# Heads of the stages of a two-layer decoder kernel: where stores are awaited, where semaphores are cleared, in which order weights are split, and two combinations reordered

## The chip, the core and the metric

One core of one Trainium2 chip runs the kernel. A core has a matmul engine (TensorE, PE in the rows), a vector engine (VectorE, DVE), a scalar engine (ScalarE, ACT), a general one (GpSimd, POOL) and one that issues DMA transfers (SyncE, SP); each has a queue of its own, and they wait for each other on semaphores. The metric is the device time of one execution in microseconds (us), lower is better.

## The reference

It computes two decoder layers over 2048 tokens of 512 numbers, here 16 batches of 128 tokens. Cut to its last lines:

```
x = _layernorm(x + _L0_attn_ref(x, ...))    # 16 heads of 128, rope, causal
x = _layernorm(x + _L0_xattn_ref(x, ctx_1024, fside, fside, ...))   # 32 heads of 16, axial rope
x = _layernorm(x + _L0_ffn_ref(x, ...))     # 32 experts, top 4, capped at 80 tokens, and a shared expert
x = _layernorm(x + _L1_attn_ref(x, ...))    # 16 heads of 32, causal
x = _layernorm(x + _L1_xattn_ref(x, ctx_1024, ...))   # 16 heads of 128, rms norm of q and k
x = _layernorm(x + _L1_ffn_ref(x, ...))     # 8 experts of 352, top 2
```

The attentions look across the tokens of groups of batches; the routed experts read packed rows of tokens and write rows, which are gathered back, weighted and summed (the combination) before the layer norm.

## The kernel before

The kernel is a row of stages, each an `nc.Block()` of its own with five instruction streams, buffers and semaphores. In the order in which they run, with the names that prefix their tiles: **a** (`wide_attention` with rope), **b** (`narrow_attention` with rope and the first router), **cd** (`late_routing`, with a part of the shared expert), **m** (`capped_experts`), **cc** (`combine_beside`: the rows of the routed experts gathered and summed, beside three quads of four batches of the shared expert on PE), **d** (`narrow_attention`, causal), **e** (`wide_attention` with rms norms and the second router), **r** (`end_of_routing`), **n** (`routed_experts`) and **fc** (`combine_last`).

Every product of fp32 matrices is made of three matmuls of halves: a number is split into a high half (a cast, `w_hi`, `x_hi`) and the rest (a subtraction, `w_lo`, `x_lo`), and `split_product` (lines 87 to 89; line 1263 in the narrow stages) multiplies high by low, low by high and high by high. So before the first product of a stage, its weights and its first row of tokens must be loaded and split. The 128x512 row x is turned by four transposes on PE (`turn_x`, lines 637 and 1253), copied and cast by ACT (lines 318, 326, 923), and its low half is made by POOL (line 392) or DVE (line 1114). Casts of weights are line 214 and 939, subtractions line 220 and, on DVE, 1123, on POOL 1043. While a head waits, PE makes `keep_busy` transposes of the identity (line 76), whose counts are the argument `busy`.

Weights of the next stages are fetched ahead by `Staged` into a shared tile `staged`; a stage with `head_ready` has its first row fetched ahead as well (`FirstTile`).

A stage ends when SP has waited for its last stores (`sp.wait_ge(out_st, ...)`); then the block's own barrier, and then `Stage.clear` at the end of the stage's context:

```
def clear(self):
    if self.used:
        self.nc.clear_and_free_semaphores(self.used)
        self.nc.all_engine_barrier()
```

That second barrier is line 50. It runs 15 times.

In cc, POOL issues four indirect DMA gathers for each of the 16 batches (line 2878) in the order `ORDER`, into four buffers; buffers must be zero first, since rows of tokens that an expert dropped are skipped. The first two are cleared by POOL (line 2869), later ones by ACT (line 2832). DVE takes a batch (four multiply-adds, line 2768) between its work for the shared expert: the hidden layer of a column block f (lines 1696, 1701), the low half of the next quad's rows (`take_x_lo`), and the sum of a finished batch (`add`, line 1705). Norms need a root, `(var + eps) ** -0.5`, made by POOL (`Combination.root`, lines 2758 and 2760); ACT applies the norm for groups of batches (line 2787), DVE for the last ones (line 2792). In fc it is the same with two gathers per batch (line 2982), eight buffers that need no clearing, and the roots of groups 0 to 2 between the gathers.

The stages' order, the order of instructions in each queue and the counts of fillers are written out by hand.

## Time and profile before

| what | value |
| --- | --- |
| median of 3 runs | 3379.65 us (3378.88 to 3382.94) |
| the profiled execution, its own time | 3378.42 us |
| its span in the profile | 3376.6 us |
| mean granted clock of PE | 0.969 of full speed |
| PE busy | 3119.7 us, 92% |
| DVE, POOL, ACT busy | 2209.4, 1556.4, 1445.5 us |
| stages a, b, cd, m | to 975, 1437, 1497, 1674 us |
| stages cc, d, e, r, n, fc | to 1800, 2140, 2970, 2993, 3311, 3375 us |

All times of rows are microseconds from the start of the span, of one execution on the only core. A row of a timeline has the start, the length, the engine, the line, the operation and what it writes and reads; `x4` means that four equal instructions in a row are put together, and the bracket says how long the engine stood idle before and what ended that. A row of waits has the total, the number and the longest. The names of instructions that issue a DMA or wait on SP carry a q (SPq): the engine's queue.

### The profile page before, as it was taken

How to read it: one execution, taken by the hardware profiler on the slowest of the kernel's cores; microseconds unless marked ns; L12 is line 12 of the kernel's file. 1: busy time of each engine (PE TensorE's matmuls, PEld its weight loads, DVE VectorE, ACT ScalarE, POOL GpSimd, SP SyncE). 2: the span in 40 equal slices, each digit the busy share in tenths (PEclk: the TensorE clock that was granted, in tenths of full speed). 3: DMA queues.
4: the chain of work that ended last, by engine and by line, in shares of the span. 5: the costliest groups of instructions: out<-in, count | busy, mean ns of one | idle time of the engine just before them, and what ended most of it. 6: DMA issues, size and time to landing. Idle time of an engine off the chain costs nothing. (4 is left out here: it accounts for less than half of the span.)

```text
span 3376.6 us, 57674 instructions
## 1 busy us (share of the span) xinstructions
PE 3119.7 (92%) x20634; PEld 2598.7 (77%) x20634; DVE 2209.4 (65%) x3889; ACT 1445.5 (43%) x3497; POOL 1556.4 (46%) x1466
## 2 busy tenths in 40 slices
PE   7999999999979999988897999799999999979992
PEld 6887888878867777775576777688888888869991
DVE  5667566567645676649785777556667678755555
ACT  3333333343336666528753333344444444324441
POOL 4544343344432333335573222345555556645555
PEclk9999999999989999989998999899999999989996
DMA  5001016022220111149612112311101001156665
GB/s 176 18 13 60 0 36 239 0 80 88 105 104 22 46 34 31 52 159 356 220 47 92 41 40 63 123 37 35 37 12 48 12 24 38 51 183 239 236 235 162
DMA packets 133268, 303.14 MB, mean 90 GB/s; under 512 B 21152, under 2 KB 33184, under 8 KB 126832
## 3 DMA queue, kind: packets, MB, share of 16 engines
q1 hardware_dynamic: 115584, 274.61, 23.7%
q0 software_dynamic: 15360, 22.16, 2.1%
q10 hardware_dynamic: 2160, 4.21, 0.4%
q8 instruction: 100, 1.64, 0.2%
q14 instruction: 64, 0.52, 0.0%
HBM read 231.07 MB, written 98.04 MB: 97 GB/s over the span
## 5 line engine op out<-in xcount | busy, mean ns | idle before, releaser
L404 POOL TENSOR_TENSOR a_sq<-a_tq,a_sinq 128x256 f32<-128x256 f32 x128 | 150.6, 1195 | 357.3 <-DVE a_tq L484 356.0
L370 ACT COPY a_probT<-bank 128x512 f32<-128x512 f32 x64 | 37.5, 586 | 327.2 <-PE bank L725 327.2
L404 POOL TENSOR_TENSOR a_sk<-a_tk,a_sink 128x256 f32<-128x256 f32 x128 | 123.7, 986 | 90.1 <-DVE a_tk L484 90.1
L417 POOL TENSOR_TENSOR e_sk<-e_tk 128x512 f32<-128x512 f32 x64 | 66.5, 1039 | 204.5 <-DVE e_tk L511 204.5
L354 ACT ACTIVATE a_sm<-a_sm,a_nmax 128x128 f32<-128x128 f32 x256 | 99.9, 391 | 122.0 <-DVE a_nmax L580 122.0
L359 ACT ACTIVATE e_prob<-bank,e_nb,e_rq 128x128 f32<-128x128 f32 x256 | 113.8, 455 | 86.3 <-DVE e_nb L585 86.3
L1061 POOL TENSOR_TENSOR d_prob<-d_prob,d_nmax 128x1024 f32<-128x1024 f32 x32 | 63.9, 1998 | 181.2 <-DVE d_nmax L1160 181.2
L967 ACT ACTIVATE b_prob<-bank,b_nb 128x128 f32<-128x128 f32 x512 | 139.0, 386 | 11.1 <-DVE b_nb L1165 11.1
L2361 POOL TENSOR_TENSOR m_down_lo<-cw_down,m_down_hi 128x1024 fp32r<-128x1024 f32 x32 | 92.8, 2901 | 106.2 <-ACT m_down_hi L2323 106.2
L506 DVE TENSOR_TENSOR a_kr<-a_kr,a_sk 128x512 f32<-128x512 f32 x64 | 66.5, 1038 | 88.9 <-POOL a_sk L404 88.9
L2607 POOL TENSOR_TENSOR n_wu_lo<-nw_wu,n_wu_hi 128x1408 fp32r<-128x1408 f32 x23 | 74.1, 3224 | 106.1 <-DVE n_wu_hi L2651 106.1
L2374 DVE TENSOR_TENSOR m_up_lo<-cw_up,m_up_hi 128x1024 fp32r<-128x1024 f32 x64 | 118.6, 1855 | 2.2 <-ACT m_up_hi L2318 2.2
L1162 DVE TENSOR_REDUCE b_nmax<-bank 128x8 f32<-128x1024 f32 x64 | 77.8, 1215 | 63.6 <-PE bank L1306 62.9
L370 ACT COPY e_probT<-bank 128x512 f32<-128x512 f32 x64 | 37.5, 586 | 183.7 <-PE bank L725 183.7
L958 ACT COPY b_probT<-bank 128x512 f32<-128x512 f32 x128 | 78.3, 612 | 87.9 <-PE bank L1315 87.9
L2612 POOL TENSOR_TENSOR n_wd_lo<-nw_wd,n_wd_hi 128x1024 fp32r<-128x1024 f32 (+1 forms) x46 | 100.7, 2208 | 28.2 <-ACT n_wd_hi L2580 28.1
L419 POOL TENSOR_TENSOR e_sq<-e_tq 128x512 f32<-128x512 f32 x64 | 66.6, 1040 | 96.2 <-DVE e_tq L515 96.2
L87 PE MATMUL bank<-a_wq_hi,a_x_lo 128*128 128x512 f32 x256 | 107.0, 418 | 4.2 <-DVE a_wq_lo L220 4.1
L392 POOL TENSOR_TENSOR a_x_lo<-a_xall,a_x_hi 128x512 fp32r<-128x512 f32 x64 | 89.8, 1403 | 41.0 <-ACT a_x_hi L326 41.0
L87 PE MATMUL bank<-a_wk_hi,a_x_lo 128*128 128x512 f32 x256 | 101.0, 394 | 6.6 <-DVE a_wk_lo L220 6.5
L87 PE MATMUL bank<-e_wo_hi,e_z_lo 128*128 128x512 f32 x256 | 106.4, 415 | 0.5 <-DVE e_z_lo L548 0.5
L87 PE MATMUL bank<-a_wo_hi,a_z_lo 128*128 128x512 f32 x256 | 105.3, 411 | 0.3 <-DVE a_z_lo L548 0.3
(578 smaller groups left out, 11130.5 us busy)
## 6 DMA issues: line engine op xcount, KB each, us to landing
packed<-all_zero SPq DMA_DIRECT2D x32, 1024.0 KB, 8.2
cw_up<-in_c_wgu SPq DMA_DIRECT2D x32, 1024.0 KB, 8.6
cw_down<-in_c_wd SPq DMA_DIRECT2D x32, 512.0 KB, 8.5
nw_wg<-in_f_wg SPq DMA_DIRECT2D x23, 704.0 KB, 5.8
nw_wu<-in_f_wu SPq DMA_DIRECT2D x23, 704.0 KB, 7.6
nw_wd<-in_f_wd SPq DMA_DIRECT2D x23, 512.0 KB, 7.3
nw_xe<-packed SPq DMA_DIRECT2D x46, 256.0 KB, 2.7
result<-n_ye SPq DMA_DIRECT2D x46, 256.0 KB, 2.0
```

Source lines behind the costliest of these rows:

```text
L87: nc.tensor.matmul(ps, a_lo, b_hi, start=start, stop=False)
L354: step = nc.scalar.activation(prob[:, j, :], sm[:, j, :], ACT.Exp, bias=nmax[:, j:j + 1], accum_out=rsum[:, j:j + 1])
L359: step = nc.scalar.activation(prob[:, j, :], pS[:, P * j:P * j + P], ACT.Exp, bias=nb[:, j:j + 1], scale=rq[:, par, j:j + 1], accum_out=rs ...
L370: nc.scalar.copy(probT[:], pP[:, :]).then_inc(act_pt, 1)
L392: sub = nc.gpsimd.tensor_tensor(x_lo[:, par].rearrange("p c t -> p (c t)"), xall[:, b, :], x_hi[:, par].rearrange("p c t -> p (c t)").bitc ...
L404: step = nc.gpsimd.tensor_tensor(o, i, s, ALU.mult)
L958: nc.scalar.copy(probT[:, s // 2 % 2, s % 2], pP[:, :]).then_inc(act_pt, 1)
L967: step = nc.scalar.activation(prob[:, p % 2, i], pS[:, i // H, P * (i % H):P * (i % H) + P], ACT.Exp, bias=nb[:, p % 2, i:i + 1], scale=SCALE)
L1162: nc.vector.tensor_reduce(nmax[:, p], scores, AX.X, ALU.max, negate=True).then_inc(v_nm, 1)
L2361: nc.gpsimd.tensor_tensor(down_lo[:, e % 2], weights.down[:, e % R], down_hi[:, e % 2].bitcast(F32), ALU.subtract).then_inc(g_down, 1)
L2374: nc.vector.tensor_tensor(up_lo[:, e % 2, part(half)], weights.up[:, e % R_UP, part(half)], up_hi[:, e % 2, part(half)].bitcast(F32), ALU. ...
L2612: sub = nc.gpsimd.tensor_tensor(o, x, y.bitcast(F32), ALU.subtract)
```

## The change

It has five parts.

**Ends of stages.** The last stores of a, cc and d (the last four of a and cc, the last one of d) and all of m signal semaphores of the whole program (`x1_out`, `x2_out`, `x3_out`, `result_out`). Their own stage no longer waits for them; the next one does, at the places shown. Ended semaphores are collected in a list `ended` and cleared in `st.block()`, at the start of the next stage, with no barrier behind; one clear and one barrier stand at the program's end.

**Constants.** Their loads move from ACT's queue to SP's in a, b, d and e. In stage a the loads of wv, `tri` and `ones` are issued later (`fetch_rest`).

**Weights and rows in the heads.** q's weight is split in four pieces of 512 columns, so that PE can begin with the first; weights are split ahead of rows. In a, wv's low half moves from POOL to DVE, behind the rotation of k, and v is projected after k's transposes. In e, the context (s) and k come first, then x, v and q.

**Fillers.** `busy` goes in a from (0, 30) to (0, 14), in b from (20, 36, 0, 34) to (0, 12, 0, 34), in d from (12, 28, 42, 30) to (20, 8, 42, 30), in e from (20, 20) to (20, 0); 16 are added in cc behind `turn_x`; the first block makes 3 warm-up matmuls in place of 9.

**Combinations.** In cc `ORDER` and the buffers' clears change, takes begin with the first column block of quad 0, and between quads DVE's order is written out (`between_downs`); roots and norms come two column blocks earlier. In fc the roots of groups 0 to 2 are made by ACT (square root) and DVE (`inverse`, six small operations that refine it) in place of POOL.

```diff
     def end(self):
+        self.ended.extend(self.used)
+    def block(self):
+        self.clear()
+        return self.nc.Block()
     def clear(self):
-        if self.used:
-            self.nc.clear_and_free_semaphores(self.used)
-            self.nc.all_engine_barrier()
+        if self.ended:
+            self.nc.clear_and_free_semaphores(list(self.ended))
+            self.ended.clear()
...
# wide_attention, SP
+                fetch_rest(sp)
...
+                router.load(sp)
+                sp.wait_ge(*stored)
                 head.fetch(sp)
...
             if keep is None:
-                sp.wait_ge(out_st, 16 * B)
+                sp.wait_ge(out_st, 16 * (B - 4))
# wide_attention, ACT
-            if rope:
-                for n in tab:
-                    act.dma_start(tab[n][:], w_dram[n]).then_inc(c_in, 16)
-                act.dma_start(bo[:], w_dram["bo"].partition_broadcast(P)).then_inc(c_in, 16)
...
+            if rms:
+                split_hi(act, nc.scalar.copy, "q", 0)
+                act.wait_ge(ctx_in, landed(0))
+                nc.scalar.copy(s_hi[:, 0], src[:]).then_inc(act_s0, 1)
+                split_hi(act, nc.scalar.copy, "v", 0)
+                take_x(0)
+                source(0, 0, 0)
# wide_attention, POOL
-            source(0, 0, 0)
-            split_lo(pool, nc.gpsimd.tensor_tensor, "v", 0)
+            if rms:
+                pool.wait_ge(act_s0, 1)
+                nc.gpsimd.tensor_tensor(s_lo[:, 0], src[:], s_hi[:, 0].bitcast(F32), ALU.subtract).then_inc(g_s0, 1)
+            else:
+                source(0, 0, 0)
# wide_attention, DVE
                     nc.vector.tensor_tensor(kr[:], kr[:], sk[:], ALU.add).then_inc(v_k, 1)
+                    if g == 0 and is_batch(b, 0):
+                        split_lo(dve, nc.vector.tensor_tensor, "v", 0)
# wide_attention, PE
+            if rms:
+                pe.wait_ge(g_s0, 1)
+                project("k", pK, s_hi, s_lo, 0, 0, 0, pe_k)
+                turn_x(0)
+                project("v", pV, s_hi, s_lo, 0, 0, 0, pe_v)
+                pe.wait_ge(g_lo, done(0))
+                project("q", pQ, x_hi, x_lo, 0, 0, 0, pe_q)
...
+                turn_q(0)
+                turn_k(0)
+                project("v", pV, s_hi, s_lo, 0, 0, 0, pe_v)
# narrow_attention, SP
+            sp.wait_ge(*stored)
             if not head_ready:
                 head.fetch(sp)
+            sp.dma_start(xres[:], x_src(0)).then_inc(r_in, 16)
# narrow_attention, DVE
-            take_x_lo(0)
-            if router:
-                router.start(dve)
-            split_lo("q")
-            split_lo("k")
+            if rope:
+                split_q_lo(0, 2)
+                take_x_lo(0)
+                split_q_lo(2, C)
+                split_lo("k")
+                if router:
+                    router.start(dve)
+            else:
+                split_q_lo(0, C)
+                split_lo("k")
+                take_x_lo(0)
# narrow_attention, PE
-            pe.wait_ge(w_lo["q"], 1)
-            project_q(0, (0, 3 * rows_of["q"]))
+            for c in range(C):
+                pe.wait_ge(w_lo["q"], c + 1)
+                project_q(0, (3 * c, 3 * c + 3))
# combine_beside
-    ORDER = (0, 1, 2, 3, 8, 4, 5, 6, 7, 12, 13, 9, 10, 11, 14, 15)
+    ORDER = (0, 1, 2, 3, 8, 9, 4, 5, 6, 7, 12, 13, 10, 11, 14, 15)
...
+            for sem, value in written:
+                pool.wait_ge(sem, value)
             for p in range(B):
-                if p < 2:
+                if 2 <= p < R:
+                    pool.wait_ge(part.w_lo[p - 2], C)
+                    nc.gpsimd.memset(got(p), 0.0).then_inc(g_cl, 1)
+                if p < R:
                     pool.wait_ge(g_cl, p + 1)
...
-                if p == 9:
+                if p == 7:
                     sums.root(pool, 0, *GROUPS[0])
...
+            def between_downs(q, p):
+                x_lo, sums_of = Q * (q + 1), Q * q
+                dve.wait_ge(part.pe_x, done(x_lo))
+                take(p, range(2))
+                part.take_x_lo(dve, x_lo)
+                add(sums_of)
+                take(p, range(2, 3))
+                part.take_x_lo(dve, x_lo + 1)
+                take(p, range(3, K))
...
-                    if q or f:
-                        take(p)
-                        moments(b)
-                        p, b = p + 1, b + 1
+                    take(p)
+                    p += 1
+                    if b < 12:
+                        moments(b)
+                        b += 1
...
-            take(p)
             for j in range(Q):
                 add(Q * last + j)
# Combination
+    def inverse(self, dve, g, first, behind):
+        vec, own, step = self.nc.vector, slice(first, behind), self.refined
+        r, t = self.rstd[:, own], self.shift[:, own]
+        dve.wait_ge(self.act_rt, g + 1)
+        step(vec.reciprocal(r, r))
+        step(vec.tensor_tensor(t, r, r, ALU.mult))
+        step(vec.scalar_tensor_tensor(out=t, in0=self.mv[:, own, 1], scalar=EPS, in1=t, op0=ALU.add, op1=ALU.mult))
+        step(vec.tensor_scalar(t, t, -0.5, 1.5, ALU.mult, ALU.add))
+        step(vec.tensor_tensor(r, r, t, ALU.mult))
+        vec.scalar_tensor_tensor(out=t, in0=self.mv[:, own, 0], scalar=-1.0, in1=r, op0=ALU.mult, op1=ALU.mult).then_inc(self.v_sh, 1)
# combine_last
-                if b in (5, 9, 13):
-                    sums.root(pool, b // 4 - 1, *GROUPS[b // 4 - 1])
...
-                if b in (6, 10, 14):
-                    sums.shifts(dve, b // 4 - 1, *GROUPS[b // 4 - 1])
+                if b in (4, 8, 12):
+                    sums.inverse(dve, b // 4 - 1, *BY_ACT[b // 4 - 1])
```

## Rows read from the trace of the kernel before

**Rows 1.** The page: span, busy time, and the span in 40 slices.

```profile
span 3376.6 us, 57674 instructions
...
PE 3119.7 (92%) x20634; PEld 2598.7 (77%) x20634; DVE 2209.4 (65%) x3889; ACT 1445.5 (43%) x3497; POOL 1556.4 (46%) x1466
...
PE   7999999999979999988897999799999999979992
```

**Rows 2.** The waits of SP, us in total, times, longest.

```profile
SPq L50 <- PEq L50: 8.3, 15, 1.2
...
SPq L769 <- DMA x<-d_yn: 2.3, 1, 2.3
...
SPq L105 <- DMA x<-a_yall: 1.7, 1, 1.7
```

**Rows 3.** PE's timeline: start, length, line, out<-in, idle before and what ended it.

```profile
31.71 0.85 PE L669 MATMUL bank<-all_ident,a_kr 128*128 128x128 f32 x4 [3.17 <-DVE a_kr L506]
...
977.89 3.85 PE L76 MATMUL bank<-all_ident 128*128 128x128 f32 x20 [8.46 <-issue]
...
982.02 4.09 PE L76 MATMUL bank<-all_ident 128*128 128x128 f32 x36
...
987.70 0.39 PE L1263 MATMUL bank<-b_wq_lo,b_x_hi 128*128 128x512 f32 x1
...
995.44 0.63 PE L1263 MATMUL bank<-b_wv_lo,b_s_hi 128*128 128x512 f32 x1
...
1787.69 0.79 PE L87 MATMUL bank<-cc_wd_hi,cc_h_lo 128*128 128x512 f32 x1 [3.76 <-DVE moe_xall L1705]
...
2151.51 2.45 PE L76 MATMUL bank<-all_ident 128*128 128x128 f32 x20
2155.55 0.50 PE L87 MATMUL bank<-e_wk_hi,e_s_lo 128*128 128x512 f32 x1 [1.59 <-POOL e_s_lo L395]
```

**Rows 4.** DVE's timeline, heads of a, b and d, and fc.

```profile
13.49 2.50 DVE L220 TENSOR_TENSOR a_wq_lo<-all_staged,a_wq_hi 128x512 fp32r<-128x512 f32 x4 [13.49 <-ACT a_wq_hi L214]
...
17.16 6.71 DVE L220 TENSOR_TENSOR a_wk_lo<-all_staged,a_wk_hi 128x512 fp32r<-128x512 f32 x4
...
985.02 2.29 DVE L1123 TENSOR_TENSOR b_wq_lo<-all_staged,b_wq_hi 128x2048 fp32r<-128x2048 f32 x1 [0.74 <-ACT b_wq_hi L939]
...
991.73 0.69 DVE L1104 TENSOR_TENSOR b_tcq<-bank,b_tab 128x512 f32<-128x512 f32 x1
...
1810.76 2.29 DVE L1123 TENSOR_TENSOR d_wq_lo<-all_staged,d_wq_hi 128x2048 fp32r<-128x2048 f32 x1 [1.11 <-ACT d_wq_hi L939]
...
3320.59 1.54 DVE L2768 SCALAR_TENSOR_TENSOR moe_xall<-fc_got,moe_weight,moe_xall 128x512 f32<-128x512 f32 x2 [9.39 <-DMA fc_got<-result,moe_rows]
...
3323.00 1.52 DVE L2768 SCALAR_TENSOR_TENSOR moe_xall<-fc_got,moe_weight,moe_xall 128x512 f32<-128x512 f32 x2
...
3366.96 1.54 DVE L2768 SCALAR_TENSOR_TENSOR moe_xall<-fc_got,moe_weight,moe_xall 128x512 f32<-128x512 f32 x2 [0.39 <-DMA fc_got<-result,moe_rows]
```

**Rows 5.** POOL's timeline, head of a, start of cc, and fc.

```profile
16.61 6.72 POOL L220 TENSOR_TENSOR a_wv_lo<-all_staged,a_wv_hi 128x512 fp32r<-128x512 f32 x4 [3.54 <-ACT a_wv_hi L214]
...
1677.02 3.55 POOL L2869 MEMSET cc_got<- 128x2048 f32 x2 [6.48 <-POOLq L50]
...
3331.26 0.61 POOL L2758 TENSOR_TENSOR fc_rstd<-fc_mv,fc_eps 128x4 f32<-128x4 f32 x1
...
3333.71 1.01 POOL L2982 DMA_INDIRECT fc_got<-result,moe_rows  x1 [0.19 <-issue]
```

**Rows 6.** ACT's timeline, head of a.

```profile
5.96 0.40 ACTq L310 DMA_DIRECT2D a_cosq<-in_a_cosq  x1
...
9.04 1.28 ACT L318 ACT_TABLE_LOAD   x1 [9.04 <-issue]
```

**Rows 7.** Windows: length, busy time of each engine, granted clock, DMA share.

```profile
1003.80:1015.30 11.50, 9.34 (x47) 7.38 (x47) 3.48 (x5) 6.42 (x19) 0.72 (x1) 0.51 0.13 36
1682.40:1704.70 22.30, 22.24 (x100) 18.42 (x101) 16.75 (x28) 13.47 (x16) 17.73 (x16) 1.00 0.49 145
```

More of the change, by code:

```diff
@@ L326, in source @@
                 copy = nc.scalar.copy(x_hi[:, par], xall[:, b, :])
-                if rms:
+                if rms and not (is_batch(b, 0) and g == 0):
                     act.wait_ge(ctx_in, landed(u))
@@ L939, in split_hi, with split_q_hi @@
                 nc.scalar.copy(hi[n][:], raw[n]).then_inc(w_hi[n], 1)
+            def split_q_hi(first, behind):
+                act.wait_ge(w_in["q"], 16)
+                for c in range(first, behind):
+                    nc.scalar.copy(hi["q"][:, c], raw["q"][:, c]).then_inc(w_hi["q"], 1)
             def take_v(b, par):
@@ L2300, in _ @@
             store(NE - 1)
-            for n in range(2):
-                sp.wait_ge(y_out[n], landed(NE // 2))
         @block.scalar
@@ L2760, in root, with roots_of @@
         self.nc.gpsimd.tensor_tensor(self.rstd[:, own], self.rstd[:, own], self.mhalf[:, own], ALU.pow).then_inc(self.g_rs, 1)
+    def roots_of(self, act, first, behind):
+        own = slice(first, behind)
+        act.wait_ge(self.v_mv, behind)
+        act.wait_ge(self.g_c, 2)
+        self.nc.scalar.activation(self.rstd[:, own], self.mv[:, own, 1], ACT.Sqrt, bias=self.eps[:, 0:1]).then_inc(self.act_rt, 1)
+    def inverse(self, dve, g, first, behind):
[8 more added lines that the diff above has]
+        vec.scalar_tensor_tensor(out=t, in0=self.mv[:, own, 0], scalar=-1.0, in1=r, op0=ALU.mult, op1=ALU.mult).then_inc(self.v_sh, 1)
     def take(self, dve, p, b, got, ks):
@@ L2893, in take @@
                 dve.wait_ge(g_in[p % R], 16 * K * (p // R + 1))
-                if first <= b and b not in (8, 12, 13, 14, 15):
+                if first <= b and b not in ROUTED_FIRST:
                     dve.wait_ge(part.v_b, done(b - first))
@@ L2905, in add @@
                 b = first + n
-                if b in (8, 12, 13, 14, 15):
+                if b in ROUTED_FIRST:
                     dve.wait_ge(sums.v_k, K * (ORDER.index(b) + 1))
                 part.add(dve, n, y(b), y(b))
+            def between_downs(q, p):
[7 more added lines that the diff above has]
+                take(p, range(3, K))
+                add(sums_of + 1)
+                take(p + 1, range(1))
+                part.take_x_lo(dve, x_lo + 2)
+                take(p + 1, range(1, 2))
+                add(sums_of + 2)
+                take(p + 1, range(2, 3))
+                part.take_x_lo(dve, x_lo + 3)
+                take(p + 1, range(3, K))
+                add(sums_of + 3)
             part.begin_vector(dve)
@@ L2959, in combine_last @@
         y_out = st.sem("y_out")
-        block = ctx.enter_context(nc.Block())
+        block = ctx.enter_context(st.block())
         @block.scalar
         def _(act):
-            for g in range(BY_ACT):
-                sums.normed_act(act, g, *GROUPS[g])
+            for g, group in enumerate(BY_ACT):
+                sums.roots_of(act, *group)
+                sums.normed_act(act, g, *group)
+            sums.normed_act(act, len(BY_ACT), *BY_POOL[0])
         @block.sync
         def _(sp):
-            behind = GROUPS[BY_ACT - 1][1]
+            behind = BY_POOL[0][1]
             for b in range(B):
```

313 lines of the change are left out of this document (178 added, 135 removed).

## The prediction

> **What bounds the kernel now.** I read the page first, for shares: TensorE (PE) is busy 3119.7 of 3376.6 us, and no other engine passes two thirds. The 40 slices say where the rest is: PE's digit is 9 nearly everywhere and falls in the first slice, around the borders of the stages, and in the last, where it is 2 [rows 1]. So time can be won only where PE stands still or runs below full clock. Next, SP's waits: what the end of a stage costs. SP sits 8.3 us in 15 second barriers (line 50), and 2.3 and 1.7 us for the last stores of d and a [rows 2]; two more rows of this kind, of cc and m, have 1.7 and 1.6. Last, the timelines of the heads, engine by engine: what PE waits for there is the low half of a weight on DVE or POOL, or a row behind it [rows 3, 4, 5].
>
> **Ends of stages.** Every second barrier but the last goes: 8.3 us in 15, less about 1 for the one that stays, 7.3. The four waits for stores go from the ends: 2.3 + 1.7 + 1.7 + 1.6 = 7.3 [rows 2]; those of n and of the output stay. The engines' own drains around each barrier lie outside SP's wait; an estimate for 14 of them is 1.0. Sum 15.6. Below, 8: every landing is still waited for, one place later. Above, 18: drains count double. Behind the new waits stand: on SP the fetch of d's first row, then the residual and the next row (it comes back in d, below); on POOL in cc the gathers, which need the routed results and have memsets ahead; on ACT and DVE only work that is wanted later. Stage b has its first row fetched ahead, and e can start with k, which needs no store. The semaphores are cleared on POOL, beside the fillers and weight splits of the others. Were that cover gone, a few tenths at 14 places would be at most 4 us.
>
> **Head of a, 7.5.** DVE's four pieces of `a_wk_lo` take 6.71 us while POOL splits wv in the same time, 6.72; the four of wq, with POOL idle, took 2.50 [rows 4, 5]. The change moves wv's split to DVE, behind k's rotation: 6.71 - 2.50 = 4.2 won before k is there. v's twelve products go behind k's transposes, and fill what is now PE's wait of 3.17 us for `a_kr` [rows 3]; so wv's split must not be late: it has the rotation's other work on POOL to cover it, and uncovered would cost its 2.5. Constants leave ACT's queue, whose six issues, from 5.96 on, hold the table load and the first copy until 9.04 [rows 6]. 3.1 us are at stake; I take 1.8, as x's transposes and wq's landing are next. Six warm-up matmuls of two passes each go from the first block: 12 at 0.19 (3.85 for 20, [rows 3]) are 2.3, of which I take 1.5, since its other engines wait for a fetch. Bounds 4.2 (the split alone) and 10.
>
> **Head of b, 4.5.** DVE takes q's bank at 991.73, and only then do rotation and scores start. DVE is busy nearly without a break from x_lo to there, apart from 0.74 us for ACT's wq_hi [rows 4]; so the end moves with its start. The 20 fillers ahead of x's transposes, 3.85 us, go [rows 3], and DVE starts with two pieces of wq before x is there: 3.85 + 0.74 - 0.1 for smaller pieces. wv stays on POOL behind ACT's tables, which move by the same. Bounds 2 (x was not what it waited for) and 6.
>
> **Head of d, 2.6.** `d_wq_lo` takes 2.29 us on DVE, after 1.11 of waiting for ACT's wq_hi; x_lo had been done when that wait began [rows 4]. After, both halves of the weights come before x: 2.29 + 1.11 = 3.4. But SP fetches x only when the stores have landed, at the end of the 1.7 booked as gone; half of that, 0.8, comes back. Bounds 0 and 5.
>
> **Head of e, 3.8.** k's first product waits 1.59 us for `e_s_lo`, behind 20 fillers of 2.45 us, and e_s_lo stands behind x's work on ACT and POOL [rows 3]. After, s and k come first, before x, and the fillers go: 1.59 + 2.45 = 4.0, less 0.2 for the wait on constants in SP's queue. q, last now, has its squares taken where k's were. Bounds 1 and 6.
>
> **cc, a loss of 1.4.** At the end PE waits 3.76 us for line 1705, which DVE reaches only after one more batch has been taken [rows 3]; that take is earlier now, and 3.8 is won. Against it: two memsets of the kind that takes 3.55 us for two [rows 5] move from ACT onto POOL, between gathers, and push the third batch and all behind it back by 3.6, while DVE now wants batches one step earlier. DVE itself has room for the extra take in quad 0 (busy 16.75 of 22.30 us, [rows 7]). Between quads two more operations of 0.77 (half of 1.54 [rows 4]) stand ahead of an x_lo: 1.6. 3.8 - 3.6 - 1.6 = -1.4. Bounds: 3.8 won (both losses covered), 9 lost (the gathers stay late in the second quad too).
>
> **fc, 5.1.** No matmul here. POOL gathers one row set in 1.25 us and stops for three roots: from 3331.26 to the next gather at 3333.71 is 2.45 [rows 5]; the other two, read in the same way, have 1.54 and 3.25. Sum 7.2, which go to ACT (idle) and DVE. Then DVE is next: from the first take at 3320.59 to the second at 3323.00 are 2.41 us, 2.45 with the gap between them; 16 batches make 39.2 [rows 4]. The three inverses are 18 operations of 4 numbers a row, which no row shows in this shape: more than nothing, less than a 512-wide one (0.77); nearer the low end, 0.22 each, 4.0. From 3320.6 that ends at 3363.8; before, the last take starts at 3366.96 and its batch ends 2.4 later, 3369.4. Won 5.6, less 0.5 for waits on gathers still in it. Bounds 2 (0.4 each) and 7.2.
>
> **Sum.** 15.6 + 7.5 + 4.5 + 2.6 + 3.8 - 1.4 + 5.1 = 37.7. The profiled execution took 3378.4 us, its span 3376.6; less 37.7 it is 3340.7. The median of the runs shown is 1.2 above it, so 3342.
>
> **The clock.** The change takes fillers away: in a 30 to 14, b 56 to 12, d 40 to 28, e 40 to 20. A 512-column product lasts 0.39 us at full clock (987.70) and 0.63 at half (995.44) [rows 3]: 0.24 for each that falls to 1.2 GHz. Behind b's head the granted clock is 0.51 for 11.5 us though PE is busy 9.34 of them [rows 7]. In b, 36 transposes take 4.09 us, 0.114 each, where the 20 before them took 3.85, 0.19 each, and the products behind start at full clock [rows 3]: fillers raise the clock. The Trainium skill (TensorE: Matmul & The Clock Gate, Part 4: PE-mode transpose) holds that transposes do not count as work for the clock. By it fillers bought nothing, and to remove them costs nothing; this trace disagrees. By the trace, fewer of them can leave first products at half clock.
>
> **Rivals.**
> 1. The clock in the heads: a, b, d, e have 36, 24, 36 and 24 products ahead of the first scores; half of these 120 at half clock are 60 x 0.24 = 14: 3356. For: 0.51 behind b's head. Against: products, not transposes, now fill the same time. 0.10.
> 2. cc held by gathers in the second quad too: 9 lost instead of 1.4: 3350. For: POOL's queue gets longer. Against: the first gather moves up with the stage's start. 0.13.
> 3. cc's gathers covered: the 5.2 of losses vanish: 3337. 0.15.
> 4. The waits only move, the change does not do what it says: the 7.3 for stores come back and half of b's, d's and e's heads, 5.5: 3355. 0.06.
> 5. Slower: half clock stays beyond the heads, as behind b's now. It takes 37.7 / 0.24 = 157 products more than now at half clock to cancel the gain, and 185 to be slower by 0.2%, 3387. Against: the stretch of low clock here is 11.5 us, not 80. Slower 0.02, within 0.2% 0.03.
> The forecast itself 0.51. 0.2% (6.8 us) is about what a measurement can tell from no change. Faster 0.95, same 0.03, slower 0.02. The range reaches from rival 3, less the upper bounds of a and b in part, 3333, to rival 1 with 1 above, 3357.
>
> **What would show it.** Right: nothing at line 50's place between stages; SP waits for no store of a, m, cc or d before a barrier; `a_wk_lo` near 2.5 us; q's bank in b taken 7 us earlier against a's last product; no roots between fc's gathers, and DVE without waits there. Wrong: granted clock near 0.5 through the heads; DVE waiting for gathers in cc's quads 1 and 2; POOL's clears ahead of what PE waits for; PE in d still waiting for x where it waited for wq_lo.

## The result, and the profile after

The changed kernel takes 3350.39 us, median of four runs (3349.58 to 3354.56), beside 3379.95 of the kernel before on the same chip (3378.88 to 3382.94): the ratio is 0.992 [0.9908, 0.9933], 29.6 us less. Forecast were 3342 and a gain of 37.7, with a range of 3333 to 3357, which holds the result. Two repeats on other chips gave 0.9921 [0.9902, 0.9939] (`again`, 3363.68 beside 3392.16) and 0.9913 [0.99, 0.9927] (`again_2`, 3352.13 beside 3381.85). So absolute times differ from chip to chip by more than most terms here; ratios and single stretches of the traces are what can be compared.

The profiled execution took 3354.56 us, its span 3352.7: 23.9 less than the span of before [rows 1]. It is the slowest of its four, and the median gains 5.7 more. The page of the changed kernel, as in [rows 1]:

```profile
span 3352.7 us, 57409 instructions
...
PE 3109.4 (93%) x20546; PEld 2588.7 (77%) x20546; DVE 2205.3 (66%) x3916; ACT 1444.2 (43%) x3511; POOL 1541.2 (46%) x1456
...
PE   8999999999989999989888999799999999979992
```

The shape is that of before. To see where 23.9 us came from I cut the span at rows of PE that both kernels have: the first scores of a stage (its first product of k and q), the last product of a stage, the first gather of fc. The table is worked out in us, from the starts of such rows, and from the end where it is a last product.

| stretch | before | after | again | again_2 | gained, forecast |
| --- | --- | --- | --- | --- | --- |
| start to a's first scores | 33.3 | 31.2 | 29.9 | 30.6 | 7.5 |
| a's last product to b's first scores | 34.4 | 27.4 | 27.4 | 27.4 | 6.8 |
| middle of b to its end | 180.8 | 183.9 | 187.2 | 183.9 | 0 |
| b's end to cd's first shared product | 15.1 | 14.0 | 14.2 | 14.0 | 0.6 |
| cd | 47.6 | 48.2 | 51.1 | 48.1 | 0 |
| cd's end to m's end | 176.3 | 173.4 | 173.8 | 173.5 | 0.6 |
| m's end to cc's first product | 9.5 | 6.0 | 6.0 | 6.0 | 2.8 |
| cc, quad 0 | 36.8 | 45.6 | 46.3 | 46.2 | |
| cc, quad 1 | 36.7 | 38.6 | 38.9 | 37.2 | |
| cc, the rest | 40.1 | 33.5 | 33.7 | 33.7 | all of cc: -1.4 |
| cc's end to d's first scores | 29.3 | 23.9 | 24.2 | 24.1 | 5.5 |
| d's end to e's first scores | 31.3 | 25.2 | 25.1 | 25.1 | 6.7 |
| e's end to n's first row | 27.5 | 25.9 | 26.0 | 26.3 | 1.2 |
| n's end to fc's first gather | 5.0 | 4.5 | 4.5 | 4.5 | 1.2 |
| fc's first gather to its last norm | 55.7 | 53.3 | 53.5 | 51.9 | 5.1 |
| last norm to the end | 5.4 | 5.3 | 5.3 | 5.3 | 1.2 |

The last column splits the 15.6 for ends of stages by their place: 0.6 for each of 14 second barriers, and the store waits of a, cc, m and d. The stretches left out (the long middles of a, b, d, e, n) differ by up to 1.8 us in either direction. Since the heads and the ends share their borders, I also read where PE's first instruction of a stage stands behind the last product of the stage before: that place shows the end alone.

**Ends of stages.** SP's waits of the changed kernel (total, times, longest), to be read beside [rows 2]:

```profile
SPq L3247 <- PEq L3247: 1.6, 1, 1.6
SPq L1567 <- DMA x<-moe_xall: 0.9, 1, 0.9
```

Of 15 barriers with 8.3 us, one with 1.6 is left; of the store waits, 0.9 comes back in front of d's first row. The borders up to cc and that of e to n gained what was forecast or more in all three executions; those to e, to fc and the program's end gained less, that to d up to 0.3 less. PE's first instruction comes 2.3 us sooner in b (6.17 behind a's last product, 8.46 before), 0.8 in cd, 0.5 in m, 2.7 in cc, 2.7 in d, 3.3 in e and 0.8 in r. With the 0.5 of fc's first gather, the 0.1 at the end and some 0.4 to 0.8 at n, which I have only as a rest, the ends of stages gave 14.1 to 14.6.

**The heads and cc.** PE's timeline of the changed kernel, beside [rows 3]:

```profile
21.18 1.09 PE L682 MATMUL bank<-all_ident,a_xin 128*128 128x128 f32 x4 [3.70 <-DMA a_xin<-in_x]
...
24.31 1.11 PE L714 MATMUL bank<-all_ident,a_kr 128*128 128x128 f32 x4 [1.19 <-DVE a_kr L544]
...
26.58 0.63 PE L96 MATMUL bank<-a_wv_lo,a_x_hi 128*128 128x512 f32 x1
...
31.24 1.06 PE L752 MATMUL bank<-a_kT,a_qT 128*128 128x128 f32 x8
...
973.65 1.08 PE L1335 MATMUL bank<-all_ident,all_first_x 128*128 128x128 f32 x4 [6.17 <-issue]
...
977.52 0.63 PE L1345 MATMUL bank<-b_wq_lo,b_x_hi 128*128 128x512 f32 x1
...
990.20 0.63 PE L1375 MATMUL bank<-all_ident,b_qs 128*128 128x128 f32 x4 [0.77 <-ACT b_qT L1017]
...
1700.22 0.79 PE L95 MATMUL bank<-cc_wd_hi,cc_h_lo 128*128 128x512 f32 x1 [6.20 <-DVE cc_h_lo L1784]
...
2146.30 0.97 PE L714 MATMUL bank<-all_ident,e_kr 128*128 128x128 f32 x4 [2.90 <-DVE e_kr L566]
```

k's transposes in a stand at 24.31 where they stood at 31.71: 7.4 earlier, the forecast to a tenth. But v's twelve products stand between them and the scores, and most of them run at half clock (0.63 each), so of 7.4 only 2.1 reach the scores. In b the first products run at half clock too (0.63 against 0.39 at 987.70, [rows 3]), and no row shows that they cost anything: DVE reads q's bank only behind its tables, and b's scores are 7.0 earlier. In cc there is a new gap of 6.20, in e one of 2.90.

DVE's timeline of the changed kernel, beside [rows 4]:

```profile
13.68 2.50 DVE L239 TENSOR_TENSOR a_wk_lo<-all_staged,a_wk_hi 128x512 fp32r<-128x512 f32 x4
17.40 0.69 DVE L522 TENSOR_TENSOR a_tq<-bank,a_bq 128x512 f32<-128x512 f32 x1 [1.22 <-DMA a_sink<-in_a_sink]
...
982.97 0.69 DVE L1175 TENSOR_TENSOR b_tcq<-bank,b_tab 128x512 f32<-128x512 f32 x1 [0.35 <-DVE b_tab L1305]
...
1694.92 3.11 DVE L2870 SCALAR_TENSOR_TENSOR moe_base<-all_staged,moe_weight,moe_base 128x512 f32<-128x512 f32 x4 [4.81 <-DMA all_staged<-result,moe_rows]
...
2142.00 0.69 DVE L555 COPY e_tq<-bank 128x512 f32<-128x512 f32 x1 [5.65 <-PE bank L97]
2142.61 0.68 DVE L557 TENSOR_REDUCE e_ssk<-e_sk 128x4 f32<-128x512 f32 x1
...
2145.10 1.14 DVE L566 SCALAR_TENSOR_TENSOR e_kr<-e_tk,e_rk,e_gg 128x128 f32<-128x128 f32 x4
...
3312.04 0.16 DVE L2858 TENSOR_TENSOR fc_shift<-fc_rstd 128x4 f32<-128x4 f32 x1
...
3319.26 1.54 DVE L2870 SCALAR_TENSOR_TENSOR moe_xall<-fc_got,moe_weight,moe_xall 128x512 f32<-128x512 f32 x2 [1.49 <-DMA fc_got<-result,moe_rows]
...
3334.97 1.54 DVE L2870 SCALAR_TENSOR_TENSOR moe_xall<-fc_got,moe_weight,moe_xall 128x512 f32<-128x512 f32 x2 [2.08 <-DMA fc_got<-result,moe_rows]
```

`a_wk_lo` takes the 2.50 forecast. In cc the third batch has not landed when DVE wants it: 4.81 us of idle time. In fc DVE stands still four times for a gather, 0.40, 1.49, 0.47 and 2.08, 4.4 together, where 0.5 had been allowed.

POOL's timeline at the start of cc, and in fc, beside [rows 5]:

```profile
1690.97 1.83 POOL L2972 MEMSET all_staged<- 128x2048 f32 x1
1693.57 1.00 POOL L2979 DMA_INDIRECT all_staged<-result,moe_rows  x1 [0.77 <-POOL all_staged L2972]
...
3313.83 1.43 POOL L3102 DMA_INDIRECT fc_got<-result,moe_rows  x1 [0.30 <-issue]
```

Each of the two memsets costs the queue more than its 1.83: the next gather starts 2.60 us after the memset does (1693.57 - 1690.97), because POOL waits another 0.77 for the write to be done. In fc no root stands between gathers any more.

### The profile page after: what moved, and what is told of

It reads as the page before. It is cut to its first block and busy times, and to the rows that moved or that the text cites. A ratio compares the mean times of both kernels' runs of the same rounds, so it can differ in the third digit from the quotient of the medians.

```text
span 3352.7 us, 57409 instructions
## 1 busy us (share of the span) xinstructions
PE 3109.4 (93%) x20546; PEld 2588.7 (77%) x20546; DVE 2205.3 (66%) x3916; ACT 1444.2 (43%) x3511; POOL 1541.2 (46%) x1456
## 3 DMA queue, kind: packets, MB, share of 16 engines
q1 hardware_dynamic: 117312, 275.67, 23.9%
## 5 line engine op out<-in xcount | busy, mean ns | idle before, releaser
L622 DVE TENSOR_REDUCE e_nmax<-bank 128x4 f32<-128x512 f32 x64 | 44.1, 689 | 97.1 <-PE bank L752 97.1
```

## The experiments

Each edit is against the changed kernel unless said. The ratio is to the kernel before on the same chip. `again`, `cc_clears_on_act`, `e_k_chain_first` and `a_v_before_turns` ran on one chip; `cc_clears_and_late_takes`, `fillers_in_the_gaps`, `second_barriers_back` and `stores_awaited_at_end` on a second, where the changed kernel itself didn't run; `again_2`, `cc_as_before`, `fc_no_early_stores` and `three_mends` on a third. Each kernel was profiled once, so a stretch is read from one execution.

### again, again_2: the changed kernel once more

> The changed kernel once more, unaltered. Its profiled execution took 3354.6 us where its other three took 3349.6 to 3350.8. Against the kernel before, by PE's instructions set side by side, it lost 3.1 us in the last 40 us of stage b while PE ran at half clock, and moved by 1.8 us steps in m, by 1.7 at the end of e and by 1 to 2 in n. If these belong to the change, the same steps stand here; if they are phases of the clock, they come and go, and the sum of the rest stays: heads of a -2.3, b -6.1, d -5.7, e -4.2, cc +4.1, fc -3.0.

> The changed kernel unaltered, as the measure for the other three of this chip. Its ratio to the kernel before was 0.992 twice; 0.990 to 0.994 again.

Measured as above: the gain is 0.8 to 0.9% on three chips. The table shows which stretches repeat to a tenth (the borders, the end of cc) and which wander by some us (the head of a, the end of b, cd, quad 1 of cc, fc).

### cc_clears_on_act: the two clears back on ACT

```diff
-                if 2 <= p < R:
-                    pool.wait_ge(part.w_lo[p - 2], C)
-                    nc.gpsimd.memset(got(p), 0.0).then_inc(g_cl, 1)
...
+                if (q, f) == (0, 0):
+                    clear(2)
+                    clear(3)
```

> One part undone: ACT clears the third and fourth gather buffer (both after the first column block), not POOL. In the changed kernel DVE waits 4.81 us for the third batch in quad 0 of cc, PE then stands 6.20 us, and the quad ends 9.2 us worse than it began. Theory M (the memsets between the gathers are the cost): the third batch's gathers start 2.3 us sooner and the fourth's 5.4, PE's gap falls from 6.20 to about 3.9, and less of the down products runs at half clock; 3 to 5 us faster in all. Theory T (the takes come too early for any gathers): PE's gap stays over 5 us, under 1 us gained. Theory A (ACT becomes the late one): its two copies of 1.9 us delay the activation of the second column block, and DVE waits for ACT there.

3356.55, ratio 0.9893 [0.9875, 0.9911] beside 0.9921 of `again`: 7.1 us less by medians, though the intervals overlap. The trace agrees by place: cc takes 113.0 us from its first product to its end, 118.9 in `again`, nearly all of it in quad 0 (42.3 for 46.3) and quad 1. Its PE timeline, where the kernel before has no gap in front of these products and the changed kernel has 6.20:

```profile
1701.70 0.50 PE L95 MATMUL bank<-cc_wd_hi,cc_h_lo 128*128 128x512 f32 x1 [1.88 <-DVE cc_h_lo L1784]
...
1709.99 0.66 PE L1794 MATMUL bank<-all_ident,moe_xall 128*128 128x128 f32 x4 [3.35 <-DVE cc_sx_lo L1763]
```

The clears on POOL cost 4 to 6 us. What is left of quad 0's loss, 42.3 against 36.8 of before, isn't the memsets. These two waits of PE, which the kernel before doesn't have, make 5.2 of the 5.5. The second is at the border of the quads: DVE waits 1.40 us for a gather there and makes two multiply-adds, 1.54, before it comes to the low half of the next row, where the kernel before makes that half first.

### cc_clears_and_late_takes: the takes of quad 0 later as well

On top of the edit above, DVE skips the take behind column block 2 and makes two behind block 3:

```diff
+                    if (q, f) == (0, 2):
+                        continue
+                    for _ in range(2 if (q, f) == (0, 3) else 1):
-                    take(p)
-                    p += 1
...
```

> The clears of the third and fourth buffer on ACT, and in quad 0 the third batch's take moved behind the last hidden block, next to the fourth's. With the clears on ACT alone, cc went from 118.9 to 113.0 us from its first up product to its end, of which quad 0 gave 4.0. If the rest of quad 0's loss is the third take standing ahead of the last hidden blocks (theory T), PE's gap ahead of the down products goes to under 1 us and cc ends another 2 to 4 us sooner. If DVE's own work is the limit now (rival), the two takes in a row only move the gap behind the down products: no gain.

3364.56, ratio 0.9923 [0.9907, 0.994]. Quad 0 takes 43.3, no better than with the clears alone. The gap has only moved to the border of the quads, as its PE timeline shows:

```profile
1706.53 1.11 PE L1794 MATMUL bank<-all_ident,moe_xall 128*128 128x128 f32 x4 [5.83 <-DVE cc_sx_lo L1763]
```

DVE must have made the same takes by that border, and the batches land when they land. The place of the takes within quad 0 is not what costs. Neither kernel changes the order at the border (`between_downs`); no run undoes that alone.

### cc_as_before: the whole combination of cc as before

`combine_beside` is that of before, with only the new handling of semaphores and last stores.

> The changed kernel with the whole combination beside the shared expert as before: order of batches, buffer clears, takes, roots and norms; the 16 fillers and the awaited stores stay. The prediction put the reordering at a loss of 1.4 us. From the first up product to the last, cc took 113.6 us before, 117.7 and 118.9 in the changed kernel. Expected by that: 113 to 115, and 3 to 5 us faster than the changed kernel. Rival (the earlier start and the fillers, not the order, made quad 0 short of gathers): 117 or more.

3352.75, ratio 0.9917 [0.9902, 0.9932], beside 3352.13 of `again_2`. In the trace cc takes 36.8 + 36.8 + 40.1 = 113.6 us, exactly before's, 3.5 less than in `again_2` and within the 113 to 115 expected; but its whole time doesn't show that, since n and fc were 2 us each longer in it. So the reordering of cc, as made, costs 3.5 to 5.3 us of its own stretch, and the whole times can't resolve it.

### e_k_chain_first: k's norm ahead of q in DVE's and POOL's queues in e

For the first batch POOL takes k's square and root before x's low half and q's square, and DVE sums, and turns out `kr`, before it reads q's bank.

```diff
# DVE, first batch
+                    dve.wait_ge(g_k, done(u))
+                    nc.vector.tensor_reduce(ssk[:], heads(sk[:], H), AX.X, ALU.add).then_inc(v_ak, 1)
+                    turned_k()
                 dve.wait_ge(pe_q, done(u))
                 nc.vector.tensor_copy(tq[:], pQ[:, :]).then_inc(v_tq, 1)
```

> The changed kernel, and in e's first unit the whole chain of k (square, sum, root, scaled rows) ahead of q's copy and of x's low half on POOL. In the changed kernel k's products end at 2134.8 and its copy is made at 2135.7, but its square waits behind x_lo on POOL (2138.8) and its sum behind q's copy on DVE (2142.6), so the scaled rows are ready at 2146.2, no sooner against the stage's start than q allows. Theory C (the order of DVE and POOL held k back, k's products first bought nothing): scores start 2.5 to 3.5 us earlier, and the whole is as much faster. Rival R (q's own chain, copy and transposes, is as long): under 1 us. Rival X (x_lo behind k's square delays q's products): slower by up to 1.

3360.79, ratio 0.9908 [0.9892, 0.9925]; e's head takes 23.0 us for 25.1, 2.0 gained, a little under the expectation. DVE's timeline now has `kr` before q's bank is read (2145.10 behind 2142.00 in the changed kernel):

```profile
2147.98 1.14 DVE L561 SCALAR_TENSOR_TENSOR e_kr<-e_tk,e_rk,e_gg 128x128 f32<-128x128 f32 x4 [1.92 <-POOL e_rk L452]
2149.82 0.69 DVE L575 COPY e_tq<-bank 128x512 f32<-128x512 f32 x1 [0.70 <-PE bank L97]
```

### a_v_before_turns: v's products and split in a where they were

```diff
+                project("v", pV, s_hi, s_lo, 0, 0, 0, pe_v)
                 turn_q(0)
                 turn_k(0)
-                project("v", pV, s_hi, s_lo, 0, 0, 0, pe_v)
...
-                    if g == 0 and is_batch(b, 0):
-                        split_lo(dve, nc.vector.tensor_tensor, "v", 0)
```

wv's low half is made by POOL again, and its load is issued early.

> Part of a's head undone: wv is fetched in the first block with wq and wk and split by POOL, and v is projected before the transposes of q and k; constants, fillers and the order of x's fetch stay as changed. In the changed kernel k's transposes come 7.4 us earlier than before, but the first scores only 2.1, as v's twelve products (4.5 us, at half clock) now stand between. Theory P (their place is the cost): k's transposes come about 3 us later than in the changed kernel, since 1 MB more is ahead of the rope tables, but scores follow at once: scores 0.5 to 2 us earlier. Rival D (transfers set this head): the tables land 3.3 us later, q's rotation with them, and POOL's split of wv, 5 to 6.7 us, stands ahead of q's rotation: scores 1 to 3 us later.

3366.58, ratio 0.9926 [0.991, 0.9943]: no difference from `again` that can be told. The scores start at 30.0, as in `again` (29.9); the changed kernel's first execution had 31.2 and `again_2` 30.6, so theory P's lower end isn't ruled out. Its rows, POOL's and DVE's and PE's, in three fences:

```profile
16.58 5.41 POOL L239 TENSOR_TENSOR a_wv_lo<-all_staged,a_wv_hi 128x512 fp32r<-128x512 f32 x4 [6.80 <-ACT a_wv_hi L230]
```

```profile
19.25 0.69 DVE L523 TENSOR_TENSOR a_tq<-bank,a_bq 128x512 f32<-128x512 f32 x1 [3.45 <-DMA a_sink<-in_a_sink]
```

```profile
28.60 0.66 PE L713 MATMUL bank<-all_ident,a_kr 128*128 128x128 f32 x4 [3.70 <-DVE a_kr L545]
```

With v's products in front, k's transposes are 4.3 later (28.60 for 24.31), held by tables that land 1.8 later behind wv's load, and by POOL, which has wv's split for 5.41 ahead of the rotation; but nothing stands behind them. The twelve products fill a wait of PE there and run at full clock, and what they no longer cost at the end k's transposes lose. Both orders come out the same.

### fillers_in_the_gaps: fillers back where PE stands still in the heads

```diff
                 project_qk(0, 0, 0)
+                keep_busy(nc, pO, ident, 28)
...
             project_k(0, (0, 3 * rows_of["k"]))
+            if rope:
+                keep_busy(nc, pP, ident, 24)
```

> The changed kernel with 28 fillers in a between k's products and the transposes of the next row (where PE stands idle 3.7 us), and 24 in b ahead of v's products (idle 3.4 us). Clock theory (heads lose by half clock behind these gaps: v's twelve products of a started every 0.43 us, b's six also): v's products run at 0.23 us, a's scores come 1.5 to 2.4 us sooner, b's 1 us. Rival (the waits for DVE and POOL set the heads, the clock only decides how long PE idles after them): a's scores within 0.5 us of where they were, the whole within 1 us.

3358.53, ratio 0.9908 [0.9891, 0.9924]. Scores start at 27.6 in a, 2.3 to 3.6 sooner than in the three executions of the changed kernel, and in b 1.1 sooner. PE's timeline:

```profile
23.70 0.66 PE L714 MATMUL bank<-all_ident,a_kr 128*128 128x128 f32 x4 [2.95 <-DVE a_kr L544]
...
24.64 0.39 PE L96 MATMUL bank<-a_wv_lo,a_x_hi 128*128 128x512 f32 x1
...
27.60 1.06 PE L752 MATMUL bank<-a_kT,a_qT 128*128 128x128 f32 x8
```

All twelve products start every 0.23 us here, and in the changed kernel the first eight or nine every 0.43: from the first to the next transposes it is 2.9 us, beside 4.8, 4.8 and 4.6. That is 1.7 to 2.0 of the difference; the rest is k's transposes, 0.2 to 0.6 sooner here and at full clock themselves, and 0.56 us for `a_wv_lo` that PE waits in two of the three. The whole time doesn't show it: other stretches of this execution were longer (quad 1 of cc 44.0 for 38.9, e's head 27.4, where PE waited 1.92 for `all_first_x`). `three_mends` has the same 28 transposes and a gap of the same length (3.05), and there the first of v's products ran at 0.63 all the same. So in one execution full clock lasted over a gap of 3 us behind fillers, and in the other it didn't.

### second_barriers_back, stores_awaited_at_end: the two halves of the ends

```diff
             self.nc.clear_and_free_semaphores(list(self.ended))
             self.ended.clear()
+            self.nc.all_engine_barrier()
```

and, in the other kernel, SP waits for `last_out` (a, cc, d) and `y_out` (m) at the end of their own stages, before the block's barrier.

> The changed kernel with one part undone: an all-engine barrier stands again behind each clear of ended semaphores, now at the head of the stage. By the prediction's term (8.3 us of SP's waiting in 15 barriers and 1.0 for the drains around them): 7 to 9 us slower than the changed kernel. Rival: the clear on POOL and the barrier lie beside ACT's and DVE's first waits for transfers in a few heads, so only half of it, 3 to 5, shows.

> The changed kernel with one part undone: SP waits for the last stores of a, m, cc and d at the end of their own stage again (the next stage's waits stay and find them landed). By the prediction's term (1.7, 1.6, 1.7 and 2.3 us, of which 0.8 came back in d): 6 to 7 us slower than the changed kernel. Rival W (the waits only move): under 2 us slower, and the heads of d and e as late as now.

3372.34, ratio 0.9947 [0.9931, 0.9964], and 3373.92, ratio 0.9936 [0.9914, 0.9957]. Against the 0.9921 of `again` that is 8.8 and 5.1 us, with intervals of some 6 us about each. The borders say more: with the barriers they are 1.9 (a to b), 0.8, 1.8, 1.0, 2.0, 1.9 and 0.3 longer than in `again`, 9.6 in all; with the stores 2.7 (a to b), 2.8, 1.6 and 2.5, 9.6 in all. SP's waits in the two kernels:

```profile
SPq L59 <- PEq L59: 6.7, 9, 1.6
```

```profile
SPq L971 <- DMA x<-d_yn: 2.3, 1, 2.3
...
SPq L2965 <- DMA x<-moe_xall: 1.7, 1, 1.7
SPq L331 <- DMA x<-a_yall: 1.7, 1, 1.7
SPq L2387 <- DMA result<-moe_base: 1.6, 1, 1.6
```

The store waits are to a tenth those of [rows 2], 7.3 together. The 9.6 hold more than the ends, though. This is how long behind the last product of the stage before PE's first instruction stands (fc: the first gather), in us:

| stage | before | `again` | barriers back | stores awaited |
| --- | --- | --- | --- | --- |
| b | 8.46 | 6.17 | 6.99 | 7.82 |
| cd | 4.25 | 3.48 | 4.25 | 3.48 |
| m | 2.11 | 1.65 | 2.11 | 1.65 |
| cc | 4.69 | 1.99 | 2.74 | 3.69 |
| d | 8.61 | 5.89 | 6.85 | 7.61 |
| e | 9.59 | 6.25 | 7.98 | 8.34 |
| r | 4.29 | 3.48 | 4.58 | 3.49 |
| fc | 5.03 | 4.49 | 4.75 | 4.50 |

The stores cost 7.2 by it, as their rows say. The barriers cost 6.9, with 0.8 at n and 0.5 at the program's end 8.1. What the borders show beyond that, 2.5 and 2.4, arises behind the start of the stage, most of it in PE's transposes. Rows of b's head, first with the barriers back, then with the stores awaited; the last one stands beside the 0.63 at 990.20 of the changed kernel:

```profile
969.95 1.09 PE L1336 MATMUL bank<-all_ident,all_first_x 128*128 128x128 f32 x4 [6.99 <-issue]
```

```profile
970.95 1.09 PE L1337 MATMUL bank<-all_ident,all_first_x 128*128 128x128 f32 x4 [7.82 <-issue]
...
987.65 1.09 PE L1377 MATMUL bank<-all_ident,b_qs 128*128 128x128 f32 x4 [0.77 <-ACT b_qT L1019]
```

Four of them take 1.09 in place of 0.63, which in b makes 1.05 us in each of the two kernels; cc's 32 transposes take 5.2 and 5.4 in place of 3.7. That level of the clock need not be the barrier's or the stores' doing: `cc_clears_on_act` and `three_mends` have b's transposes at 1.09 as well, and `e_k_chain_first` has cc's at 5.4. Both halves are real and of about one size, and neither wait came back elsewhere.

### fc_no_early_stores: fc without the stores of its first 14 batches

This kernel doesn't write the first 14 batches of the output.

```diff
-                sp.dma_start(x_dst[b], base[:, b, :]).then_inc(y_out, 16)
+                if b >= behind:
+                    sp.dma_start(x_dst[b], base[:, b, :]).then_inc(y_out, 16)
```

> The changed kernel, but in fc the stores of the first 14 batches of the output are left out; only the last two are stored, so the output is incomplete. Of the prediction's 5.1 us for fc 2.4 came, as DVE still waits for gathers to land: 1.49 us and 2.08 us, each behind a burst of output stores. Theory S (the stores crowd the gathers): these waits go and the last norm comes 3 to 4 us sooner after the first gather (53.3 us now). Theory L (landing lags in any case, as 2.29 us of waiting in the kernel before stood ahead of any store): under 1 us sooner.

3350.60, ratio 0.9903 [0.9888, 0.9918]. From the first gather to the last norm it takes 50.6 us, beside 53.3, 53.5 and 51.9. DVE's waits for gathers, behind the first take, are 0.42, 0.51 and this one:

```profile
3321.91 1.54 DVE L2870 SCALAR_TENSOR_TENSOR moe_xall<-fc_got,moe_weight,moe_xall 128x512 f32<-128x512 f32 x2 [0.63 <-DMA fc_got<-result,moe_rows]
```

1.6 us in place of 4.4. That overstates it, as the changed kernel's own execution is a long one: in the twelve traces here whose fc is that of the changed kernel, these waits come to 2.9 to 5.4 us and the stretch to 51.9 to 54.0 (2.9 and 51.9 in `again_2`, on the same chip). This one lies below all twelve, with 1.6 and 50.6. So the stores of finished batches lengthen fc by 1.3 to 3.4 us; theory L's under 1 us doesn't fit, theory S's 3 to 4 is at the upper end, and part of the waits stays without any store.

### three_mends: clears on ACT, k's chain first, fillers in the gaps

The edits of `cc_clears_on_act`, `e_k_chain_first` and `fillers_in_the_gaps` together.

> The changed kernel with the three edits that won in their own place: clears of the third and fourth buffer on ACT in cc (cc 5.8 us shorter), k's chain first in e (2.0), and fillers in the gaps of a and b (2.3 and 1.1). If the places are independent the sum is 11 us less than the changed kernel, a ratio to the kernel before near 0.989. Rival: half of it is lost to phases of the clock in the long bodies between: 4 to 7 us.

3346.62, ratio 0.9891 [0.9875, 0.9907] beside 3352.13 and 0.9913 of `again_2`: 5.5 us less, half of the sum of the three, within the rival's 4 to 7. It is the fastest of all kernels here by median, 35.2 below its own before; that it beats the changed kernel rests on medians and on cc, since the intervals overlap. By place: cc 111.7 for 117.1, 5.4 won. e's head 24.6 for 25.1: only 0.5 of the 2.0, since x landed late in this execution, where `e_k_chain_first` has no such wait. Its PE timeline:

```profile
2129.86 0.66 PE L699 MATMUL bank<-all_ident,all_first_x 128*128 128x128 f32 x4 [1.69 <-DMA all_first_x<-x]
```

The heads of a (29.9 for 30.6) and b (27.5 for 27.4) show next to nothing of the fillers.

## Why the prediction was right, and where it was 8 us too high

**The whole.** The terms that fell short (head of a, cc, head of e, fc, the two last ends) add up to 10 to 13 us in the three traces, and the profiled execution's gain of 23.9 is 13.8 below the forecast. By medians it is only 8.1 below, since the profiled execution of the changed kernel was 4.2 slower than its median and that of before 1.5 faster. So the number came nearer than its terms did, and that much of it is luck.

**Ends of stages, 15.6: right.** The places named are empty. By the start of the next stage they gave 14.1 to 14.6, and put back one by one they cost 8.1 and 7.2, 15.3 together, for 8.3 and 7.3. Rival 4 (the waits only moved) is ruled out; 0.9 came back before d, where 0.8 had been taken off. Where two second barriers stood at the program's end and behind n, the 2.4 forecast brought 0.6: n's end to fc's first gather gained 0.5, the last norm to the end 0.1.

**Head of b, 4.5: right.** With its border 7.0 measured for 6.8; PE's first instruction is 2.3 of it, which leaves 4.7 for the head. q's bank in the changed kernel is read at 982.97, 8.76 before its old time [rows 4]; a's last product lies 1.95 earlier, which leaves 6.8. **Head of d, 2.6: right**; with its border 5.5, 5.2 and 5.3 for 5.5, and 2.5 to 2.8 without the 2.7 of its end.

**Head of a, 7.5: 2.1 to 3.5.** The step that failed is "v's twelve products go behind k's transposes, and fill what is now PE's wait of 3.17 us for `a_kr`". That wait is *ahead* of k's transposes. Products moved behind them fill no wait; they are put between k and the scores. The 7.4 were won at k's transposes, and 5.3 given back between them and the scores, where v's products take 4.8 us, 2.0 of that by half clock; 0.56 more is PE's wait for `a_wv_lo`. Put back ahead of the transposes (`a_v_before_turns`) they fill a wait but win nothing either, as k then comes later. A gap of PE stands ahead of it all, and SP's timeline of the changed kernel shows its cause:

```profile
9.21 2.04 SPq L3194 DMA_DIRECT2D all_tri<-in_tri  x1
...
12.19 0.54 SPq L314 DMA_DIRECT2D a_xin<-in_x  x1
```

`a_xin`, the row that PE's 3.70 at 21.18 waits for, is issued behind wv, `tri` and `ones`, 4.2 us of issues. The prediction moved the constants' cost off ACT and in a didn't price SP's queue, onto which all of it went. No run here puts them back, so how much of the 7.5 they cost or gave isn't shown.

**cc, -1.4: -3.5 to -5.3.** The mechanism and its sign were right and both sizes off. The loss in quad 0 alone was 9 us, where 5.2 had been forecast for all of cc: two memsets hold the gathers back by 2.6 each, and DVE takes each batch one step sooner. `cc_clears_on_act` gives the memsets 4 to 6; the rest, 4 to 6 in quad 0, stays with the clears mended. In the rows of `cc_clears_on_act` it is PE's 1.88 and 3.35, and of the 3.35 some 1.5 are the two multiply-adds ahead of an x_lo that the prediction had priced at 1.6 for all of cc. The rest I put down to the demand for one more batch there, which gathers that start every 1.3 to 1.6 us can't meet; that is argued, since no kernel here asks for one batch less alone, or undoes the order between the quads alone. "DVE itself has room for the extra take" was true and not the question. The end of cc gained 6.5, not 3.8. Rival 2, 9 lost, was right of the first quad alone.

**Head of e, 3.8: about 2.9.** With its border 6.1 for 6.7, of which 3.3 is the end. s and k did come first, but k's chain then waits its turn in two queues: its square behind x_lo on POOL, its sum (2142.61) behind q's bank on DVE (2142.00), which itself waits for twelve products of q. `e_k_chain_first` gives 2.0 more. The prediction followed PE's order and not that of the two engines behind it.

**fc, 5.1: 2.2 to 3.9.** "less 0.5 for waits on gathers still in it" was the term at fault: 4.4, and 2.9 to 5.4 over all traces. `fc_no_early_stores` puts 1.3 to 3.4 us down to the stores, by one execution without them. The inverses cost less than forecast: 18 operations of 0.14 to 0.17 us that start every 0.2, some 3.2 in place of 4.0.

**The clock.** Rival 1 (half clock in the heads, 14 us) came in small part: 1.7 to 2.0 by v's products in a, while the first ones in b delayed nothing that a row shows. v's products in b ran at 0.63 in the kernel before too [rows 3], and `fillers_in_the_gaps` won 1.1 there. One loss lay where no edit is. Windows of the end of b (length, busy time and count of PE, PEld, DVE, ACT, POOL, granted clock, DMA share, GB/s), first in before, then in the changed kernel, then in `again`:

```profile
1403.00:1413.00 10.00, 9.09 (x134) 7.71 (x134) 8.81 (x19) 6.25 (x20) 3.97 (x5) 1.00 0.10 28
1413.00:1423.00 10.00, 7.98 (x110) 6.17 (x107) 6.86 (x25) 5.66 (x18) 4.05 (x6) 1.00 0.08 15
```

```profile
1395.00:1405.00 10.00, 9.23 (x102) 7.82 (x100) 8.88 (x18) 4.78 (x15) 3.06 (x4) 0.83 0.11 28
1405.00:1415.00 10.00, 8.72 (x102) 6.81 (x101) 4.65 (x20) 6.15 (x20) 4.19 (x4) 0.83 0.02 3
```

```profile
1395.00:1405.00 10.00, 9.00 (x86) 7.32 (x86) 7.99 (x17) 4.37 (x13) 3.06 (x4) 0.63 0.11 28
1405.00:1415.00 10.00, 9.19 (x81) 7.51 (x78) 3.44 (x6) 5.07 (x16) 4.19 (x4) 0.69 0.02 2
```

The stretch holds the same instructions in all three, with the same gaps ahead of them (0.84, 0.74 and 0.77 us), and the granted clock is 0.83 and 0.83, 0.63 and 0.69, where before had 1.00. 0.17 of 20 us is 3.4, and the stretch is 3.1 longer; 0.37 and 0.31 of 10 us each are 6.8, and it is 6.4 longer. The reverse, in m's second half, is windows of before, then of the changed kernel:

```profile
1620.00:1650.00 30.00, 28.40 (x143) 18.69 (x142) 25.33 (x28) 24.97 (x42) 17.86 (x6) 0.96 0.95 341
1650.00:1672.00 22.00, 19.47 (x88) 12.39 (x87) 13.14 (x18) 13.13 (x24) 10.57 (x5) 0.92 0.18 54
```

```profile
1610.00:1640.00 30.00, 26.78 (x141) 17.59 (x140) 28.55 (x30) 24.84 (x41) 16.38 (x7) 1.00 1.01 368
1640.00:1664.00 24.00, 21.65 (x108) 13.91 (x106) 16.12 (x20) 15.70 (x28) 13.56 (x5) 1.00 0.19 60
```

0.04 of 30 and 0.08 of 22 are 3.0, where the stretch is 2.5 to 2.9 shorter, 0.5 of it by the barrier ahead of m. Why the clock fell in the one place and not in the other stays open: before was profiled once, and no run here changes one of these stretches alone. The two cancel in the profiled execution.

## What to carry to other kernels

When an instruction is moved to fill a wait, write down on which side of the wait's own instruction it lands; behind it, it fills nothing and is one more step to the end. For each load that leaves one queue, price what it now stands ahead of in the other, and follow a value that is wanted sooner through every queue it passes, not PE's alone. Cleaning up between stages (semaphores, a second barrier, waits for stores that another stage can make) was the surest of all edits here: each half gave what its rows in the list of waits say. To tell such a gain from that of the head behind it, read where the next stage's first instruction stands, not only its first scores.

## What the hardware did that I had not expected

- A store wait in SP's rows is worth its length at the next stage's start: 7.2 us for four of 7.3. The same edit read at the first scores shows 9.6, since the transposes behind it ran at half clock in that execution (four in 1.09 us, in place of 0.63).
- The granted clock of an untouched stretch can differ by a quarter between two executions (0.63 and 0.83, with the same instructions and gaps), worth 3.3 us between them; full clock lasted over a gap of 3 us behind 28 transposes in one execution and not in another.
- Behind a memset the next gather of the same engine starts 0.77 us after its end; two memsets of 1.83 held the gathers back by 5.2.
- Operations of 4 numbers a row take 0.14 to 0.17 us on DVE, and start every 0.2.
- Stores of finished batches lengthen the waits for gathers beside them: 1.6 us of waits without the first 14, 2.9 to 5.4 in twelve executions with them.
